# Dispatch stage: eight places for gathered rows instead of four, and six experts' gathers ahead of the first scatter

## The reference

```
def _L3_ffn_ref(x, Wr, W1, W2):            # B, S, D, F, E = 8, 256, 128, 512, 8
    cap = 256                              # ceil(2048 * 1.0 / 8)
    xf = x.reshape(t, d)
    probs = softmax(xf @ Wr)
    eidx = argmax(probs);  p_tok = probs[eidx]
    rank = position of the token among the tokens of its expert
    keep = rank < cap
    dispatch[e, slot] = token, valid[e, slot] = keep
    xe = xf[dispatch]                      # gather, 8 x 256 rows
    h  = maximum(einsum('ecd,edf->ecf', xe, W1), 0)
    ye = einsum('ecf,efd->ecd', h, W2) * p_tok[dispatch] * valid
    y  = zeros.at[dispatch].add(ye)        # scatter
# last line of the reference:
x = x + tanh(g_ffn[3]) * _L3_ffn_ref(_layernorm(x), Wr, W1, W2)
```

## Time and profile before

| | us |
|---|---|
| median of three runs | 929.79 |
| the profiled execution's own time | 931.02 |
| its span, first to last instruction | 929.3 |
| first gather issued, from the span's start | 869.78 |
| last scatter issued, from the span's start | 919.60 |

### The profile page before, as it was taken

One profiled execution on the slowest core, in us unless ns is written; L12 is line 12 of the kernel. 1 busy time (PEld: TensorE's weight loads), 2 busy tenths in 40 slices (PEclk: granted clock), 3 DMA queues, 4 the chain that ended last, 5 costly groups with the idle time before them and its releaser, 6 DMA issues. The chain is left out here.

```text
span 929.3 us, 14695 instructions
## 1 busy us (share of the span) xinstructions
PE 761.3 (82%) x4955; PEld 519.0 (56%) x4955; DVE 629.1 (68%) x1757; ACT 408.2 (44%) x896; POOL 374.9 (40%) x537
## 2 busy tenths in 40 slices
PE   3576999936898989897899699889999989886473
PEld 1555888814444445443535676557754457665363
DVE  4765322247788887773799976888967778994421
ACT  2034444403666666676244065435530047664310
POOL 6154334167655554500485333221101036543363
PEclk9967999976999999999999989999999989987697
DMA  7604776610000000000000000000010050001320
GB/s 195 266 26 133 205 218 201 206 38 9 15 14 13 12 7 2 1 1 1 1 0 1 1 1 1 1 1 1 1 69 0 22 160 2 23 24 45 91 55 28
DMA packets 52635, 48.59 MB, mean 52 GB/s; under 512 B 6900, under 2 KB 47751, under 8 KB 52306
## 3 DMA queue, kind: packets, MB, share of 16 engines
q1 hardware_dynamic: 49010, 40.06, 14.3%
q0 software_dynamic: 3552, 7.61, 3.0%
HBM read 38.47 MB, written 9.37 MB: 51 GB/s over the span
## 5 line engine op out<-in xcount | busy, mean ns | idle before, releaser
L1738 DVE TENSOR_REDUCE scratch<-psum 128x2 f32<-128x512 f32 (+1 forms) x160 | 106.6, 684 | 36.4 <-PE psum L1445 22.1
L1656 ACT ACTIVATE scratch<-psum 128x512 f32<-128x512 f32 x160 | 94.4, 603 | 67.3 <-PE psum L1465 67.3
L237 POOL TENSOR_SCALAR veps<-moments 128x4 f32<-128x4 f32 (+1 forms) x52 | 10.6, 205 | 239.9 <-DVE moments L158 238.2
L318 ACT ACTIVATE XT<-psum 128x512 f32<-128x512 f32 (+1 forms) x40 | 22.2, 561 | 119.6 <-PE psum L303 119.5
L941 DVE SCALAR_TENSOR_TENSOR scratch<-psum,b_block_bias,scratch 128x256 f32<-128x256 f32 (+1 forms) x48 | 18.6, 429 | 70.9 <-ACT scratch L1103 65.8
L1013 POOL DMA_INDIRECT scratch<-pair_rows,b_gather_at x39 | 39.2, 1005 | 65.2 <-PE psum L1157 42.3
L2616 PE MATMUL psum<-late,scratch 128*128 128x512 f32 x128 | 55.3, 592 | 0.0
L1465 PE MATMUL psum<-scratch,arena 128*128 128x256 bf16 x256 | 49.6, 276 | 5.4 <-ACT scratch L1636 4.4
L303 PE MATMUL psum<-ident,XN 128*128 128x128 f32 x144 | 27.8, 322 | 30.9 <-DVE XN L169 25.6
L1445 PE MATMUL psum<-arena 128*128 128x512 bf16 x128 | 50.8, 402 | 1.2 <-DVE scratch L1738 1.2
L240 POOL TENSOR_TENSOR rstd<-veps,minus_half 128x4 f32<-128x4 f32 (+1 forms) x52 | 49.1, 945 | 6.7 <-POOL veps L237 0.2
(11 more groups left out here) (471 smaller groups left out, 2042.6 us busy)
## 6 DMA issues: line engine op xcount, KB each, us to landing
arena<-in_L_ffn_w SPq DMA_DIRECT2D x72, 128.0 KB, 3.1
arena<-in_L_ffn_wg SPq DMA_DIRECT2D x24, 256.0 KB, 3.2
wide<-in_L_xattn_Wkv SPq DMA_DIRECT2D x1, 2048.0 KB
wide<-in_L_ffn_W SPq DMA_DIRECT2D x1, 2048.0 KB, 8.8
late<-in_L_ffn_W SPq DMA_DIRECT2D x8, 256.0 KB, 6.3
pair_results<-scratch SPq DMA_DIRECT2D x15, 128.0 KB, 3.5
folded_values<-arena SPq DMA_DIRECT2D x3, 512.0 KB, 4.7
scratch<-folded_values SPq DMA_DIRECT2D x3, 512.0 KB, 4.8
```

Of the source, the lines that this page charges most:

```text
L1656: a.activation(out, bank[3 + e % 2][:, :], ACT.Exp).then_inc(s["exp"], 1)
L1738: v.tensor_reduce(out, bank[m % 3][:, :].rearrange("p (h t) -> p h t", t=n), AX.X, ALU.max, negate=True).then_inc(s["maxed"], 1)
```

## The change

The stage gets a place for each of the eight experts (`ROWS = 8`), so no place is used twice. A gather no longer waits for `copied`. Its wait for `turned` stays, because the four semaphores that count the gathers' landing are still used in turn. `AHEAD` goes from 4 to 6. The arithmetic, the DMAs and the instruction order of PE, DVE, ACT and SP are the same.

```
     SLOT_TILES = E * TILES
+    ROWS = 8
     RING = 4
-    AHEAD = 4
+    AHEAD = 6
...
-        R, T = self.RING, self.SLOT_TILES
+        R, T = self.ROWS, self.SLOT_TILES
         self.rows = sc.take(R * 2 * self.CAPACITY).rearrange("p (u i k d) -> p u i k d", u=R, i=self.TILES, k=2)
...
             if e >= self.RING:
                 g.wait_ge(s["turned"], e - self.RING + 1)
-                g.wait_ge(s["copied"], self.TILES * (e - self.RING + 1))
             for i in range(self.TILES):
                 at = self.TILES * e + i
-                g.indirect_dma_start(self.rows[:, e % self.RING, i, :, :].rearrange("p k d -> p (k d)"), None, self.given,
+                g.indirect_dma_start(self.rows[:, e, i, :, :].rearrange("p k d -> p (k d)"), None, self.given,
...
-                                       c.gates[:, 7:8], self.rows[:, e % self.RING, i, 1, :],
+                                       c.gates[:, 7:8], self.rows[:, e, i, 1, :],
...
-                last = t.transpose(c.bank[6 + e % 2][:, i * P:(i + 1) * P], self.rows[:, e % self.RING, i, 0, :], c.ident[:])
+                last = t.transpose(c.bank[6 + e % 2][:, i * P:(i + 1) * P], self.rows[:, e, i, 0, :], c.ident[:])
```

## The result

The changed kernel takes 920.88 us, the median of four runs (918.99 to 922.85), against 930.07 us (929.17 to 930.99, four runs) for the kernel before on the same chip. The ratio is 0.9898, with a 95% interval of 0.9876 to 0.9920. Forecast were 920.8 us, and 919.1 to 923.7 as the range.

A forecast was written before the change was run, and what follows sets the result against it. POOL's 32 DMA issues at about 1.30 us were taken to bound the last stage once never idle; filling four gaps saves 9.03 us, taken as 9.0: 929.79 - 9.0 = 920.8 us, range 919.1 to 923.7.

The forecast's parts named there:

- The two-way wait of PE and POOL: Last 80 us: PE's `turn` waits for gathered rows, 12.9 us; POOL's scatters wait for DVE's `add`, 10.5 us.
- The places give nothing by themselves: Gathers on POOL: lifting the wait for `copied` counts zero; eight places only allow the order to change.
- 9.03 us less: POOL's last stage: four long gaps, 10.23 us in all, shrink to 0.30 each, moving its last issue to 910.6.
- PE at 3.74 us for an expert, `turn(7)` never late: PE's last stage: 3.74 us per expert if rows are there; `gather(7)` lands 1.1 us ahead of its `turn`.
- 0.2 us of slack for expert 6: POOL's tail: `scatter(6)` may go at 906.5, its turn comes at 906.7, so no wait for DVE.
- Rival 1: Last stage: a gather lands late and PE stays the bound; 922.4 to 923.7 us, chance 0.09.
- Rival 2: POOL: issue is not a bound, scatters go once their add is done; 918.5 us, chance 0.03.
- Rival 3: PE runs at 1.2 instead of 2.4 GHz from 888.5 on; slower, 936.0 us, chance 0.02.
- Rival 4: POOL: a wait counted as met is not; half the gain 925.3 us, none 929.8; chance 0.04, half no change.
- the two ways of counting: POOL's last stage: removing the long gaps gives 9.03 us less; counting 30 steps of 1.30 gives 9.3 less.

The follow-up runs named there:

- all gathers first: Changed kernel with all sixteen gathers ahead of the first scatter (AHEAD = 8): 920.33 us, ratio to the kernel before 0.9901.
- four scatters less: Changed kernel without the scatters of the second tile of experts 0 to 3: 921.66 us, ratio to the kernel before 0.9909.
- nineteen transposes: Changed kernel with nineteen transposes of the identity on PE ahead of `turn(0)`: 921.09 us, ratio to the kernel before 0.9903.
- five ahead: Changed kernel with five experts' gathers ahead of the first scatter instead of six (AHEAD = 5): 924.34 us, ratio to the kernel before 0.9932.
- eight more gathers: Changed kernel with eight extra gathers into unused scratch columns, two behind the scatters of each of experts 2 to 5: 931.80 us, ratio to the kernel before 1.0022.

## Why the prediction was right

- *The two-way wait of PE and POOL.* Shown. Five places of waiting for rows became one, and of the waits for DVE 0.19 us are left on POOL.
- *The places give nothing by themselves.* Shown by the places alone (ratio 0.9990, interval with 1). What they buy, 5.4 to 6.0 us of the stretch, they buy through the order, which the order alone shows.
- *9.03 us less.* Measured 8.98. The four gaps of 10.23 us are one of 0.49 and three of 0.30, and POOL's busy time is 0.16 us shorter (32.18 against 32.34). The last scatter came 40.84 us after the first gather, forecast 40.8. That the two agree to 0.05 us is in part luck: the wait of 0.19 us, which the sum put at nothing, and the shorter issues nearly cancel.
- *PE at 3.74 us for an expert, `turn(7)` never late.* Measured 3.74; the gathers landed in 2.8 us in the median and 3.8 at most (estimated from the earlier trace rows as 3.0 and 3.9).
- *0.2 us of slack for expert 6.* It was not there: POOL waited 0.19 us. PE's chain came 0.2 us later than forecast, since `first(0)` took 3.39 us and not the 3.17 of the trace before, and POOL's turn came 0.1 us earlier. In three experiments in which PE's last 32 products began 0.4 us later after the first gather (34.22, 34.22 and 34.28 us with all gathers first, four scatters less and nineteen transposes, against 33.84, and `first(0)` at 3.77 or 3.78 us), the stretch is 0.4 us longer. This is the one place where a small error counted.
- *Rival 1* (a late gather): not in the changed kernel; with five ahead it happens, at `turn(6)` and `turn(7)`, for 0.48 and 1.48 us.
- *Rival 2* (issue is no bound): refuted by eight more gathers at 1.33 us each. The Trainium skill, "DMA: Bandwidth & Descriptors", section "Anatomy of one DMA", on which that rival rested, calls descriptor generation small and variable. The trace does not agree that issuing is small: each of these indirect DMAs behind the first kept POOL busy for 0.98 to 1.05 us. Whether that time goes into the descriptors no run here tells, since all of them move 128 rows.
- *Rival 3* (the lower clock throughout): the clock was 1.00 from 878 on. *Rival 4*: the waits for `turned` were met, as the gaps of 0.30 at `gather(4)` (877.36) and `gather(5)` (879.96) show.
- *Two readings that were off without consequence.* `turn(1)` had ended 4 us ahead of need in the trace before, not 2. And `scatter(2)` could not go near 890: `add(2)` started 21.1 us after the first gather in the changed kernel, which would be 890.9 on the time axis of the trace before. Its turn on POOL, 26.4 us after the first gather, came later still.

What else was a matter of luck: the profiled execution after lies 12 us below the one before, 3 us more than its last stage explains. The medians of four, 9.19 us apart, agree with the stage; but their interval, 0.9876 to 0.9920, reaches from 7.4 to 11.5 us less, so the total alone could not have confirmed a sum to a tenth.

## What to carry to other kernels

Where two engines wait for each other in turn, add up each one's issues without the gaps; the larger sum is what a better order can reach, and here it gave the answer within 0.4 us (40.5 or 40.8 by the two ways of counting, 40.84 measured). A buffer that is freed earlier is worth nothing until the order behind it changes, and an order that runs ahead is worth only part, here 3 to 4 of 9 us, until the buffers are there. Once the two sums meet, shortening either one alone gives next to nothing (0.25 us and none here), so look at both before the next edit.

## What the runs showed of the hardware

An indirect DMA of 128 rows costs POOL 1.30 us in a train of its kind, for gathers as for scatters (1.29), and 1.32 to 1.33 on average where they alternate in pairs, in all traces of this case.

PE's clock did not rise during transposes of the identity: granted 0.50 over 866 to 870 us with PE busy for 3.40 of 4.00 us, and 1.00 only from 874 on, during the products that followed. Why is not settled; other operands, or more work of another kind, were not tried.

How much of `first(0)` ran at the lower clock differed from profile to profile, each time behind PE's wait for the first rows. Over `first(0)` the granted clock was 0.62 in the trace before (3.17 us), 0.58 in the changed kernel (3.39 us) and 0.51 with all gathers first (3.78 us), and 1.00 in the microsecond behind it. In the new order these tenths reach the end of the stage.

The start of the last stage moved by 7 us between profiles (first gather at 864.64 to 871.69), with the same instructions ahead of it. The spread is there early: the first gather of line 1036, in the second stage, was issued at 187.8 us in the changed kernel and at 192.6 in one of the experiments. Differences of 1 us in this kernel's time are therefore better read from a stretch of the profile than from the total.
